# Each of POOL's four sums of a block waits for the one before it by POOL's own signal, in the second sequence

## The reference

```python
x = layernorm(x + linear_attention(x, Wq, bq, Wk, bk, Wv, bv, Wo, bo))
x = layernorm(x + cross_attention(x, ctx, wq, wk, wv, wo, bo))
x = layernorm(x + mixture_of_experts(x, router_w, router_b, w1, b1, w2, b2))

def cross_attention(x1, x2, wq, wk, wv, wo, bo):
    q, k, v = heads(x1 @ wq.T), heads(x2 @ wk.T), heads(x2 @ wv.T)
    attn = softmax(einsum('bhnd,bhmd->bhnm', q, k) * 32 ** -0.5, axis=-1)
    return merge(einsum('bhnm,bhmd->bhnd', attn, v)) @ wo.T + bo
```

## Time and profile before

| | |
|---|---|
| median of 3 runs | 1866.66 us (1865.8 to 1867.45) |
| profiled execution | 1869.96 us |
| its span, first to last instruction | 1867.9 us |
| TensorE busy | 1843.9 us, 99% |
| TensorE weight loads | 1290.6 us, 69% |
| VectorE (DVE) busy | 1256.4 us, 67% |
| ScalarE (ACT) busy | 878.9 us, 47% |
| POOL (GpSimd) busy | 850.0 us, 46%, of which the sums L2286 584.8 us |
| chain that ended last | TensorE 86%, VectorE 9%, DMA 2% |
| mean granted clock of TensorE | 0.996 of full speed |

### The profile page before, as it was taken

The page is one execution under the profiler, slowest core; times in us unless marked ns, Lnnn a source line. Parts: engine busy times, 40 slices in busy tenths (PEclk is TensorE's granted clock), DMA queues, the critical chain, the costliest instruction groups (busy, mean ns, idle before and its releaser), DMA issues.

```text
span 1867.9 us, 27863 instructions
## 1 busy us (share of the span) xinstructions
PE 1843.9 (99%) x10488; PEld 1290.6 (69%) x10488; DVE 1256.4 (67%) x2339; ACT 878.9 (47%) x1587; POOL 850.0 (46%) x822
## 2 busy tenths in 40 slices
PE   9999999999999999999999999999999999999998
PEld 7786688788655555555555554554469998899986
DVE  6675574278787888888798799778554444344457
ACT  4322323322665666666465465457624443344433
POOL 4002201100598999998677577676122223222232
PEclk9999999999999999999999999999999999999999
DMA  8003535684767586858554443451244454534544
GB/s 289 24 1 118 186 103 178 199 243 144 170 139 168 130 202 130 176 112 178 109 135 114 103 118 87 112 115 63 79 148 127 132 142 107 141 91 131 145 111 155
DMA packets 124502, 250.19 MB, mean 134 GB/s; under 512 B 11312, under 2 KB 29504, under 8 KB 119680
## 3 DMA queue, kind: packets, MB, share of 16 engines
q1 hardware_dynamic: 109696, 187.56, 34.3%
q0 software_dynamic: 14672, 60.85, 16.0%
HBM read 148.46 MB, written 62.42 MB: 113 GB/s over the span
## 4 chain that ended last, share of the span: by engine, by line
PE 86%; DVE 9%; DMA 2%; issue 1%; POOL 1%; SPq 0%; ACT 0%; DVEq 0%; POOLq 0%; ACTq 0%
PE banks L1225 35%; PE banks L1540 12%; PE banks L1413 11%; PE banks L1424 11%; PE banks L1394 10%; DVE max L1758 5%; PE banks L1448 4%; PE banks L1231 2%; DMA raw<-in_x_t 1%; DVE den_t L1780 1%; PE banks L1325 1%; DMA k_half<-in_xwk_t 0%; DMA k_stack<-k_parts 0%; POOL x_nat L2297 0%; DVE hot_row L1936 0%
## 5 line engine op out<-in xcount | busy, mean ns | idle before, releaser
L2286 POOL TENSOR_TENSOR probs<-probs,probs 128x512 f32<-128x512 f32 x464 | 584.8, 1305 | 194.1 <-PE banks L1424 193.1
L2164 ACT ACTIVATE probs<-banks 128x512 f32<-128x512 f32 x1024 | 517.6, 626 | 286.9 <-PE banks L1413 286.4
L1758 DVE TENSOR_REDUCE max<-banks 128x1 f32<-128x512 f32 x1024 | 626.2, 680 | 37.4 <-PE banks L1394 37.0
L1413 PE MATMUL banks<-q_stack,k_stack 98*128 98x512 f32 x1024 | 403.3, 407 | 0.1
L1394 PE MATMUL banks<-k_stack,q_stack 98*128 98x512 f32 x1024 | 400.1, 398 | 1.4 <-DVE den_t L1780 1.1
L1413 PEld LDWEIGHTS banks<-q_stack,k_stack 98*128 98x128 f32 x1024 | 191.0, 187 | 151.7 <-issue 101.1
L1424 PE MATMUL banks<-probs,v_grp 128*32 128x512 f32 x2048 | 252.3, 605 | 0.0
L1394 PEld LDWEIGHTS banks<-k_stack,q_stack 98*128 98x128 f32 x1024 | 192.6, 188 | 48.5 <-DVE max L1758 13.5
L2344 POOL DMA_INDIRECT y_rows<-eo,tok x35 | 69.8, 1994 | 172.3 <-DVE eo L1991 116.2
L1424 PEld LDWEIGHTS banks<-probs,v_grp 128*32 128x32 f32 x2048 | 60.3, 110 | 118.3 <-issue 112.0
L1978 DVE TENSOR_TENSOR hid_lo<-hid,hid_hi 128x640 fp32r<-128x640 f32 x64 | 52.8, 824 | 126.3 <-ACT hid_hi L2233 126.3
(11 more groups left out here) (273 smaller groups left out, 2795.8 us busy)
## 6 DMA issues: line engine op xcount, KB each, us to landing
k_stack<-k_parts SPq DMA_DIRECT2D x144, 256.0 KB, 5.4
probs<-probs POOLq DMA_DIRECT2D x36, 1024.0 KB, 10.1
w_raw<-in_L_ffn_w SPq DMA_DIRECT2D x16, 2048.0 KB, 8.4
q_stack<-q_parts SPq DMA_DIRECT2D x48, 256.0 KB
v_grp<-v_rows SPq DMA_DIRECT2D x48, 256.0 KB, 3.5
raw<-in_ctx_t SPq DMA_DIRECT2D x8, 1024.0 KB, 6.6
k_parts<-out_hi SPq DMA_DIRECT2D x32, 256.0 KB, 2.5
k_parts<-out_lo SPq DMA_DIRECT2D x32, 256.0 KB, 3.2
```

What stands on the lines that cost most here:

```text
L1413: nc.tensor.matmul(out, keys_of(t)[0:STK + SHIFT, j, tile_of(s)], queries_of(t)[:, j, :], start=True, stop=True).then_inc(scored.sem, 1)
L1758: V.reduce_max(max4[:, tiles_of(t), :, :][:, k, j, mc:mc + 1], bank(bank_of["max", t, mc, k, j]), AX.X) \
L2164: S.activation(probs_of(t, s)[:, j, :], bank(bank_of["score", t, s, j]), ACT.Exp, scale=SCALE) \
L2286: G.tensor_tensor(a[:, j, :], a[:, j, :], b[:, j, :], ALU.add).then_inc(pair_added.sem, 1)
```

## The change

One condition is added to `add_head`. In turns of the second sequence (`groups[turns[t][0]][0]` is the sequence's number), the sums of heads 1, 2 and 3 of a block wait for the signal of the sum of the head before. The four sums work on different quarters of the two tiles; none reads what another writes.

```diff
                 a, b = probs_of(t, s - 1), probs_of(t, s)
                 pool.wait_ge(*exp_done[t, s, j])
                 pool.wait_ge(*num_summed[t, s - 1])
+                if groups[turns[t][0]][0] and j:
+                    pool.wait_ge(*pair_added[t, s, j - 1])
                 G.tensor_tensor(a[:, j, :], a[:, j, :], b[:, j, :], ALU.add).then_inc(pair_added.sem, 1)
```

## The result

The changed kernel takes 1874.68 us (median of 6 runs, 1873.22 to 1874.94), the kernel before beside it 1866.23 us (6 runs): a ratio of 1.0044, 95% interval [1.0031, 1.0057]. Slower, as forecast, but by 8.4 us where 4.9 were predicted. A second comparison of the same two kernels, the last experiment, gives 6.0 us.

What follows compares the result with a forecast made beforehand. It took VectorE, side operations included, to bound the second sequence where routing operations stand. Held operations summed 3.6 + 0.3 + 0.5 + 0.4 + 0.1 = 4.9 us onto the 1866.66 median: 1871.6 us, range 1866.5 to 1877.5.

Steps and rivals of the forecast that it cites:

- my 15 operations: VectorE's two-input SBUF operations on the second sequence's chain, held to the end of POOL's work; 4.9 us in sum.
- Readers by semaphore: TensorE's denominators and others waiting for POOL's results: cost nothing until a block's delay passes 1.25 us.
- Blocks without side work: Second-sequence blocks without routing operations on VectorE: a sign that they keep 6.57 to 6.6 us.
- The cost of a wait: Before each later POOL sum: 0.12 us a wait, 0.36 a block; the satisfied exponential wait costs nothing.
- rival C: On POOL: a second wait on one instruction costs more, 0.24 us a wait, 9.6 us, 1876.3; chance 0.10.
- 5.38 us for four: Sign in the changed profile: a block's four POOL sums take 5.38 us instead of 5.02.
- POOL's tail operations: Four small operations at the program's end, each waiting for the one before; their 0.08 us pause priced the wait.
- 13.4 block delays: The 4.9 us sum over VectorE's held operations, expressed as about 13.4 full block delays of 0.36 us.
- Rivals A: On POOL: its own signal is too cheap to matter; 0.04 us a wait gives 1.6 us, 1868.3; chance 0.24.
- L1713 is off the chain: VectorE's L1713 at 943.96 and 1254.79: same delay, but costing nothing because VectorE idles in the block behind.
- Rival B: VectorE's L1869 at 1103.96 gets in during POOL's pause: 1.0 us back, 3.8 left, 1870.4; chance 0.14.
- its rule: Chained VectorE operations take the same time with a semaphore after each or only the last; on POOL, 1866.7 us.

Runs made afterwards that it cites:

- experiment 1: Kernel before plus the three waits only in 32 second-sequence blocks where no side operation would be held longer by their sums; 1866.38 us, ratio 0.9999.
- experiment 8: Changed kernel, but POOL's first sum of blocks (8, 15), (13, 15) and (9, 13) also waits until VectorE's string is through; 1871.3 us, ratio 1.0025.
- experiment 3: Kernel before plus the waits in 49 of 52 blocks, all but (8, 13), (9, 11) and (13, 13); 1868.26 us, ratio 1.0006.
- experiment 6: Changed kernel, but a block's first sum waits for the last exponential, leaving the other three only POOL's own signal; 1864.49 us, single run.

## Why the prediction was right or wrong

**Right:** direction and mechanism. VectorE's operations in SBUF are held to the end of POOL's sum, and that, no semaphore, is what the change costs (experiments 1 and 8). But that the slowdown is clear of the noise is luck: the 49 blocks with 14 of my 15 operations come to +1.7 us in the loop, which the plain comparison can't tell from nothing (experiment 3), and the rest came from crossings that I had put at nothing. Readers by semaphore have cover enough: costed at nothing, measured nothing in the 32 blocks of experiment 1. Blocks without side work keep 6.57 us, POOL's idle time takes the delay, the first sequence is unchanged.

**The cost of a wait, wrong by half.** Taken 0.12 us, measured 0.18. The own signal itself does cost 0.12 (experiment 6). I costed the satisfied wait for the exponential at nothing and missed that two waits on one instruction cost 0.06 more; rival C had named just this and put it too high. "5.38 us for four" should read 5.57. POOL's tail operations wait for one thing only and could not show it.

**The 15 operations, fewer and smaller than listed.** At 0.55 us a block my 13.4 block delays would have given 7.4 us, some 6 of it outside the five large terms, but the blocks there grew by 3.9. (Rivals A and C use the 13.4 in the same way; five of the starts lie behind POOL's end by a fixed amount, so the list gives nearer 7.9 at 0.55.) Pairs of durations before and after, from VectorE in order of time: L1876 pays in full (0.28 to 0.84, 0.35 to 0.85), and so does L1720 (0.47 to 0.98). L1905 pays 0.34 twice, L1936 at 1008 0.32 and at 1150 0.25, L1884 at 1121 0.38, L1922 at 1143 0.13. But L1884 at 966 and 1277 (0.52 to 0.54, 0.49 to 0.52), `hot_row` at 1001 (0.67 both times) and L1713 at 1092 (0.18 to 0.23) pay nothing to speak of. Whether an operation is held longer depends on where it stands against POOL once everything ahead of it has moved, and my list took every place from the trace of before. One was new: L1876 at 1108.62, 1.0 us behind the end of the fourth sum before, grew from 0.17 to 0.62, since the gain at L1869 brought it forward into that sum.

**"L1713 is off the chain", wrong, and the largest error.** I looked for idle time of VectorE in the block behind and found it, 0.38 us at 948.38. But between L1713 and that idle time lie six short operations, and 0.48 us behind the start of the last is POOL's next first sum. A shift of 0.49 us puts it past that. Each such crossing costs not the shift alone but nearly a whole sum with it, as L1854 takes 1.26 us instead of 0.16: 1.46 + 1.45 + 1.69 = 4.6 us for three. My sum moved every end of a collision and never asked whether an operation would cross a beginning. With the 0.36 us that I believed in, L1713's string would have kept its place (experiment 6: 8.64); so there the error in the wait's price and this one multiply. L1922's string crosses even then (experiment 6: 8.39), and I had listed L1922 at 0.36 us and left it at that: for that block the right price of a wait would not have saved the sum.

**Rival B happened,** as worked out: -1.0 in block (11, 7). It has a twin that I missed: `hot_row` at 1157.81, which I had counted as 0.36 us later, got ahead of `den_s`, and the block fell by 1.35. Together they are 2.4 us back. The Trainium skill's rule (page "SBUF — State Buffer", section "Who interferes with whom") is that the order of issue decides who blocks. I had used it for B alone. The traces agree with it in all five large terms: L1854 0.03 us behind a sum's start takes 1.26 us instead of 0.16, and `hot_row` 0.15 us ahead of `den_s` makes POOL pay.

**Rival A** and its rule fall: on POOL, a wait for its own signal is not free. The page of the Trainium skill that the rule came from, "VectorE: DVE Perf Modes", section "The DRAIN you can't avoid", speaks of VectorE alone, and the runs here say nothing against it there.

**The size of the total:** 1871.6 predicted, 1874.68 and 1874.45 measured. By terms: +4.6 for three crossings (predicted 0.4, for L1922 alone), -2.4 at the two gains (predicted a loss of 0.5), +3.9 for the rest (predicted 4.1). That the rest fits is chance: a longer delay, fewer operations. What is left of the first comparison's 8.4 beyond 6.1 is not in the loop and lies within that comparison's interval; the runs of the second, at equal clock, are 6.2 apart. Whether the clock made it is not shown.

## What to carry to other kernels

Where two engines hold each other up without a semaphore, a shift of the one has a price in steps: nothing, or its own length, until a short operation crosses the start of a long one, and then nearly the long one's whole length on top. So list for each string of short operations how far its last one is from the other engine's next start, in both directions, and compare the shift with those distances before summing durations. And price a wait by rows in which the instruction already has as many waits as it will have.

## What was not expected of the hardware

- A second, satisfied wait on one instruction of POOL costs 0.06 us (four sums 5.57 us with two waits on each later sum, 5.38 with one, 5.02 with only the satisfied one).
- Operations of VectorE with one tensor operand in SBUF can be held as well: `slot_row` L1928 (tensor with a constant, a kind that the prediction had reckoned with) 1.28 us instead of 0.17, and a plain copy of 128x8, L1931, 1.11 instead of 0.17. Not all are: MAX8 of the kernel before, below, began 0.12 us behind the start of the third sum, and its four pieces are as short as elsewhere, 0.15 to 0.17 us; RECIPROCAL L1904 takes 0.18 us within a sum. The maxima (0.65 to 0.69 us) and the transposes L1780 (0.67 to 0.72) that read PSUM are not held.

```profile
1105.20 0.37 DVE L1872 MAX8 top<-rt_lg 128x8 f32<-128x8 f32 x4
```

- VectorE can hold POOL: `den_s` took 0.69 us instead of 0.24 when `hot_row` began 0.15 us before it.
- After a wait of 2.48 us TensorE ran at 1.2 GHz for 6.8 us in one profile, and in another, after 2.5 us in the same place, it did not. Twelve of the 14 profiles have one or two other such stretches, 3.4 or 6.8 us long, always near 602 us (7 profiles) or between 1309 and 1320 (11), there beside an idle time of TensorE of 1.39 us that all 14 have; a last one of 6 to 9.5 us stands at the end of all 14. The mean clock of a run, 0.994 to 0.999, goes with most of the 6 us by which runs of one kernel differ.
